# Attention scores from stacked bf16 parts or from fp32 strips, in a two-layer kernel on one core

## What is computed

```python
# "raw" attention (kind A): 16 heads of width 8
att = jnp.einsum('nqd,nkd->nqk', qm, km)
att = jax.nn.softmax(att, axis=-1)
att_out = jnp.einsum('nqk,nkd->nqd', att + batch_pos, vm)
# "cell" attention (kind B): 8 heads of width 16, in six nodes one after the other
scores = jnp.einsum('bqhd,bkhd->bhqk', qh, kh) / jnp.sqrt(dh)
attn = jax.nn.softmax(scores, axis=-1)
ctx = jnp.einsum('bhqk,bkhd->bqhd', attn, vh).reshape(B, S, d)
```

## Time and profile before

| | us |
|---|---|
| median of 3 runs (1749.43 to 1760.54) | 1758.84 |
| the profiled execution, its own time | 1754.03 |
| span in that profile, first to last instruction | 1752.0 |
| busy: TensorE (PE) / VectorE (DVE) | 1246.1 / 1222.1 |
| busy: ScalarE (ACT) / GpSimd (POOL) | 770.1 / 465.1 |
| mean granted TensorE clock | 0.827 of full speed |

### The profile page before, as it was taken

How to read it: one execution, slowest core, us unless ns; L and a number is a source line. 1 busy time by engine, 2 the same in 40 slices (tenths; PEclk the granted TensorE clock), 3 DMA queues, 4 the chain that set the end, 5 groups by cost and what they waited for, 6 DMA issues and landing times.

```text
span 1752.0 us, 25484 instructions
## 1 busy us (share of the span) xinstructions
PE 1246.1 (71%) x8542; PEld 816.5 (47%) x8542; DVE 1222.1 (70%) x2380; ACT 770.1 (44%) x1684; POOL 465.1 (27%) x399
## 2 busy tenths in 40 slices
PE   6544577568878687869876886868786988478327
PEld 5222244334655356635663465535563566246216
DVE  4212345499859975898679875898589866976774
ACT  0222255354626464446435462646444644443322
POOL 4002002323230413142223323042324222421160
PEclk9966699686988798868987798869896898579759
DMA  4125523512470346133451247034623344122102
GB/s 144 25 34 55 60 37 44 64 17 46 59 119 6 37 80 90 39 36 68 59 78 22 52 62 108 5 37 80 87 42 36 66 56 66 18 55 62 44 1 63
DMA packets 151439, 94.52 MB, mean 54 GB/s; under 512 B 43104, under 2 KB 133232, under 8 KB 151184
## 3 DMA queue, kind: packets, MB, share of 16 engines
q1 hardware_dynamic: 151312, 92.90, 34.2%
HBM read 44.88 MB, written 3.42 MB: 28 GB/s over the span
## 4 chain that ended last, share of the span: by engine, by line
PE 37%; DVE 31%; DMA 10%; issue 10%; ACT 6%; SPq 5%; POOL 1%; DVEq 0%; POOLq 0%; ACTq 0%
DVE hb L1498 8%; PE px L985 5%; PE scores_t L825 5%; PE px L997 5%; PE ps L805 5%; PE attn_out L838 4%; DVE rowmax_B L1347 4%; DMA w_e<-in_w_e 4%; DVE hb L1493 4%; DMA qks<-parts_b 3%; SPq L589 2%; DMA qks<-maxrow_B 2%; ACT probs L1091 2%; DVE rowmax_A L1347 2%; DVE work L1467 2%
## 5 line engine op out<-in xcount | busy, mean ns | idle before, releaser
L1347 DVE TENSOR_REDUCE rowmax_B<-ps 128x2 f32<-128x512 f32 x384 | 246.4, 684 | 139.7 <-PE ps L805 138.5
L1091 ACT ACTIVATE probs<-scores_t 128x512 f32<-128x512 f32 x512 | 286.9, 594 | 100.6 <-PE scores_t L825 98.5
L805 PE MATMUL ps<-qks 96*128 96x256 bf16 x768 | 166.0, 326 | 154.1 <-DMA qks<-parts_b 95.0
L825 PE MATMUL scores_t<-qks 98*128 98x256 bf16 x768 | 162.8, 318 | 43.5 <-ACT probs L1091 31.2
L997 PE MATMUL px<-ze,w_e 128*128 128x256 f32 x512 | 144.9, 417 | 59.0 <-DMA w_e<-in_w_e 54.6
L1633 POOL TENSOR_TENSOR parts_b<-rem_b,parts_b 128x256 bf16<-128x256 f32 x96 | 90.7, 948 | 347.5 <-ACT parts_b L1059 347.3
L805 PEld LDWEIGHTS ps<-qks 96*128 96x128 bf16 x768 | 69.3, 109 | 228.4 <-DMA qks<-parts_b 101.2
L1498 DVE TENSOR_TENSOR_SCAN hb<-da,hb 128x1024 f32<-128x1024 f32 x64 | 164.1, 2565 | 2.2
L1584 DVE SCALAR_TENSOR_TENSOR work<-hb,px 128x512 f32<-128x512 f32 x128 | 86.1, 682 | 112.8 <-ACT hb L1218 112.7
L1083 ACT ACTIVATE maxrow_B<-ps 8x256 bf16<-8x256 bf16 x96 | 35.5, 370 | 243.6 <-PE ps L813 242.4
L985 PE MATMUL px<-w_e,work 128*128 128x128 f32 x1024 | 134.9, 288 | 8.0 <-DVE work L1584 7.6
(11 more groups left out here) (277 smaller groups left out, 2324.9 us busy)
## 6 DMA issues: line engine op xcount, KB each, us to landing
qks<-parts_b SPq DMA_DIRECT2D x288, 128.0 KB, 4.9
w_e<-in_w_e SPq DMA_DIRECT2D x128, 256.0 KB, 3.2
stage_a<-parts_a SPq DMA_DIRECT2D x96, 64.0 KB
pos<-t_scr SPq DMA_DIRECT2D x8, 264.0 KB, 13.8
qks<-maxrow_B SPq DMA_DIRECT2D x96, 4.0 KB
probs<-in_b_we_t SPq DMA_DIRECT2D x1, 1280.0 KB, 6.0
x_in<-in_x SPq DMA_DIRECT2D x8, 128.0 KB, 3.1
v_scr<-va_fm SPq DMA_DIRECT2D x8, 128.0 KB, 12.8
```

The source lines that it names most:

```text
L805: mm = pe.matmul(o[:, qc * L:(qc + 1) * L], q(STACK, qc * P, P), k(STACK, 0, L), start=True, stop=True)
L825: mm = pe.matmul(scores_t[unit % 2][:, kc * L:(kc + 1) * L], k(STACK + 2, kc * P, P), q(STACK + 2, 0, L), start=True, stop=True)
L1091: act.activation(probs[:, group % 2, h % 4, :, :].rearrange("p a b -> p (a b)"), scores_t[unit % 2][:, :], ACT.Exp).then_inc(s_exp, 1)
L1347: dve.tensor_reduce(out=top[:, :, h], in_=parts_of(bank(b, ("max", kind, n))), axis=AX, op=ALU.max).then_inc(max_done[kind].of(b), 1)
```

## The change

Queries and keys stay fp32. Four heads lie in four strips of 32 partitions (16 features used in kind B, 8 in kind A, and the next row holds the maxima on the query side and -1 on the key side), and eight fp32 products with 16 (or 8) rows, issued strip after strip, fill four PSUM banks: four heads at once. The projections therefore make 2 x 128 columns in place of 128. The parts, the remainders, the stacking DMAs and the reordering copies are gone; so are the bf16 parts of the maxima. For the raw attention the projections go to DRAM and come back as eight DMAs in pieces of 64 bytes. VectorE reduces two heads (128x1024) at a time, ScalarE takes the exponential of two heads at a time. The four banks (`strips`, two tiles of two banks) serve the maxima and the scores in turn, and there is one set of them: `take_strips` waits for both readers of the product before. `px` is gone: layer 1 takes its banks from the three `ps`, in one round with the attentions. All places in the order are new.

```diff
-    CELL += [("q", _c), ("q1", _c), ("q2", _c), ("stack", _c, 0), ("stack", _c, 1), ("stack", _c, 2)]
-    CELL += [("max", "B", _c * BH + _h) for _h in range(6)] + [("rows", "B", 2 * _c)]
-    CELL += [("max", "B", _c * BH + _h) for _h in range(6, BH)] + [("rows", "B", 2 * _c + 1)]
-    CELL += [("score", "B", _c, _h) for _h in range(BH)]
+    CELL += [("q", _c)]
+    for _g in (2 * _c, 2 * _c + 1):
+        CELL += [("max", "B", _g), ("top", "B", _g, 0), ("top", "B", _g, 1), ("rows", "B", _g)]
+    for _g in (2 * _c, 2 * _c + 1):
+        CELL += [("score", "B", _g), ("exp", "B", _g, 0), ("exp", "B", _g, 1)]
...
-        scores_t = [ctx.enter_context(nc.psum_tensor(f"scores_t{i}", [P, 512], F32)) for i in range(2)]
+        strips = [ctx.enter_context(nc.psum_tensor(f"strips{i}", [P, 2 * 512], F32)) for i in range(2)]
...
-        px = [ctx.enter_context(nc.psum_tensor(f"px{i}", [P, 512], F32)) for i in range(2)]
...
+            def a_write(b):
+                sp.wait_ge(*qkv_a_done.at(b, 1))
...
+                sp.dma_start(bass.AP(tensor=a_scr.tensor, offset=0, ap=[[L, P], [A_PITCH * L, 3], [1, L]]), qkv_a[:, :, :]).then_inc(a_written.of(b), 16)
...
+            def gathered(i, first, heads, features):
+
+                return bass.AP(tensor=a_scr.tensor, offset=i * A_PITCH * L + 16 * first, ap=[[16, heads], [L, 16 * features], [1, 16]])
...
+                for g in range(A_GROUPS):
+                    for i, x in enumerate((qs["A"][g], ks["A"][g])):
+                        sp.dma_start(x[:, :].rearrange("p (c r) -> p c r", c=CB), gathered(i, AG * g, AG, STRIP)).then_inc(stacked_a.of(b), 16)
...
+                for g in range(2):
+                    mm = pe.matmul(o[:, g * L:(g + 1) * L], wmk[:, c, g, :], nt[:, b % 2, nk, :], start=True, stop=True)
+                mm.then_inc(s_ps, 1)
...
+            def take_strips(b, *phase):
+
+                at = STRIP_AT[(b, *phase)]
+                if at:
+                    user, was, kind, g = STRIP_LIST[at - 1]
+                    for i in range(2):
+                        if was == "max":
+                            pe.wait_ge(*top_done[kind].at(user, 2 * g + i))
+                        else:
+                            pe.wait_ge(s_exp, EXP_AT[user, kind, g, i] + 1)
+
+            def strip(tiles, b, kind, g, j, rows, first, n):
+                part, span = slice(STRIP * j, STRIP * j + rows), slice(first, first + n)
+                return tiles["B"][b % 2][part, g % 2, span] if kind == "B" else tiles["A"][g][part, span]
...
+                take_strips(b, "max", kind, g)
                 for qc in range(2):
-                    mm = pe.matmul(o[:, qc * L:(qc + 1) * L], q(STACK, qc * P, P), k(STACK, 0, L), start=True, stop=True)
-                mm.then_inc(s_ps, 1)
+                    for j in range(4):
+                        o = strips[j // 2][:, (2 * (j % 2) + qc) * L:(2 * (j % 2) + qc + 1) * L]
+                        mm = pe.matmul(o, strip(qs, b, kind, g, j, rows, qc * P, P), strip(ks, b, kind, g, j, rows, 0, L), start=True, stop=True)
+                mm.then_inc(s_strips, 1)
...
+            def exp(b, kind, g, i):
+                strips_ready(act, b, "score", kind, g)
...
+                act.activation(probs[:, group % 2, 2 * i:2 * i + 2, :, :].rearrange("p h a b -> p (h a b)"), strips[i][:, :], ACT.Exp).then_inc(s_exp, 1)
...
+                dve.tensor_reduce(out=rowmax[kind][:, b % sides_n, k % 2, 2 * i:2 * i + 2, :], in_=strips[i][:, :].rearrange("p (h q t) -> p h q t", h=2, q=2),
+                                  axis=AX, op=ALU.max).then_inc(top_done[kind].of(b), 1)
...
-            def reorder(b):
...
-                pool.tensor_copy(qsa[0:PARTS * AW, :].rearrange("p (n r c) -> p n r c", n=AH, c=CB), src).then_inc(reordered.of(b), 1)
```

More of the change, by code:

```diff
@@ L35 @@
 GELU_A, GELU_B = 0.7978845608028654, 0.044715
-CHUNK = 4
 RING = 3
@@ L90 @@
 ON = {
-    "sync": "load stack rows t_rows a_stack pos v_write v_read o_write o_read weights store",
+    "sync": "load rows t_rows a_write a_stack pos v_read o_write o_read weights store",
     "tensor": "prep_t q k v max rows score values post_b post_a ctx node aproj values_a gather wo_y ab_t ff_y "
               "z_t inproj bcdt state x2 h_t ffn ffn_out router expert expert_y",
-    "scalar": "prep_t q q1 k k1 v rows score out ctx node aproj a1 values_a gather ab_t "
+    "scalar": "prep_t q k v rows exp out ctx node aproj values_a gather ab_t "
               "z_t inproj xc bcdt sp_u sp_z state h_t ffn ffn_t router expert",
-    "vector": "prep_stats prep_apply q1 k1 a1 max post_b post_a end_y end_apply end_x wo_y wo_apply ff_y ff_apply "
+    "vector": "prep_stats prep_apply top post_b post_a end_y end_apply end_x wo_y wo_apply ff_y ff_apply "
               "n0_stats n0_apply n1_stats n1_apply n2_stats n2_apply inproj conv xc bc sp_u sp_z state y x2 ffn ffn_t ffn_out router rank expert expert_y",
-    "gpsimd": "prep_root xn_bo q2 k2 a2 reorder end_root end_scale wo_root ab_t ff_root att n0_root n1_root n2_root n0_apply conv sp_z state x2",
+    "gpsimd": "prep_root xn_bo end_root end_scale wo_root ab_t ff_root att n0_root n1_root n2_root n0_apply conv sp_z state x2",
 }
 START = {
[L104 to L107, removed]
+    "cell": [0, 24256, 48447, 72656, 96862, 121064, 145226, 169427],
+    "side": [814, 25027, 49237, 73418, 97637, 121825, 146010, 170205],
+    "raw": [193, 24399, 48624, 72826, 97064, 121238, 145411, 169627],
+    "one": [212, 24423, 48614, 72824, 96997, 121183, 145339, 169276],
 }
@@ L116 @@
+        "one": [130550, 134861, 138785, 142283, 143837, 145068, 145232, 145663, 146602],
     },
     "tensor": {
-        "cell": [-13098, -12947, -11035, -11004, -10774, -10451, -10198, -10171, -9965, -9628, -9218, -8915, -8743, -8653, -8243, -8242, -7928, -7369,
[6 rows of a table removed]
[L125 to L128, removed]
@@ L512, in hybrid_layers @@
         OUT_AT = {x: i for i, x in enumerate(OUT_LIST)}
-        REM_LIST = {which: [(b, s[1]) for b, s in order("vector") if s[0] == which + "1"] for which in "qk"}
         CTX_LIST = [(b, s[1]) for b, s in order("vector") if s[0] == "post_b"]
-        assert [k for k in UNIT] == [(b, *s[1:]) for b, s in order("scalar") if s[0] == "score"]
+        assert [(*x[:1], *x[2:], i) for x in STRIP_LIST if x[1] == "score" for i in range(2)] == list(EXP_AT)
         assert [k[:3] for k in GROUP if k[3] == 0] == OUT_LIST
@@ L771, in keys @@
                 o = take(b, ("k", c))
-                pe.matmul(o[:, 0:L], wmk[:, c, :], nt[:, b % 2, nk, :], start=True, stop=True).then_inc(s_ps, 1)
+                for g in range(2):
+                    mm = pe.matmul(o[:, g * L:(g + 1) * L], wmk[:, c, g, :], nt[:, b % 2, nk, :], start=True, stop=True)
+                mm.then_inc(s_ps, 1)
             def values_in(b, c):
@@ new lines, in scored, with queries @@
+            def scored(b, c):
+                if c:
+                    strips_ready(act, b, "score", "B", 2 * c - 1)
+                elif b >= 2:
+                    strips_ready(act, b - 2, "score", "B", 2 * NODES - 1)
+            def queries(b, c):
+                ready(act, b, ("q", c))
+                scored(b, c)
+                for g in range(2):
+                    act.activation(qs["B"][b % 2][:, g, :], bank(b, ("q", c))[:, g * L:(g + 1) * L], ACT.Identity, bias=bias_q[:, c, g:g + 1]).then_inc(q_done.of(b), 1)
@@ L1061, in values_in, with keys @@
+            def keys(b, c):
+                ready(act, b, ("k", c))
+                scored(b, c)
+                for g in range(2):
+                    act.activation(ks["B"][b % 2][:, g, :], bank(b, ("k", c))[:, g * L:(g + 1) * L], ACT.Identity, bias=bias_k[:, c, g:g + 1]).then_inc(k_done.of(b), 1)
             def values_in(b, c):
@@ L1753, in layouts @@
     put("be", f["L0_ffn_be"].T)
+    put("minus", -(np.arange(P) % STRIP == BW).astype(np.float32)[:, None])
     put("a_bq", f["L0_attn_bq"][cd][:, None])
```

523 lines of the change are left out of this document (211 added, 312 removed), and 13 rows, old and new, of the table PLACES.

## The result

The changed kernel takes 1826.66 us (median of 4 runs, 1824.24 to 1831.10) against 1758.32 us: a ratio of 1.040, 95% interval 1.036 to 1.044. It is 4% slower where the prediction said 1680 us and faster. The profiled execution has a span of 1827.1 us, 75 us more than the one before.

A forecast was written before the change was run, and what follows sets the result against it. No engine was taken as full: DVE bounds the scan, PE the next stretch, with waits between. From 1754 us, setup +9, fill -50 and seven intervals of -5 (-35) gave 1678, stated as 1680 us, range 1610 to 1950.

The forecast's parts named there:

- DMA: Per interval: weight wait gone -10, or moved to the rows of maxima +5; -5 taken, plus -4 for PE's stack waits.
- third rival: No change: the DMA convoy takes from the rows what it gave the weights, fill only -30; about 1755 us, chance 0.12.
- a period above 195 us: Sequence-to-sequence distance that would prove the prediction wrong; near 184 us was expected, 189.5 us before.
- first rival: Slower: one set of strips makes PE's queue wait for DVE or ACT at hand-overs; 1825 us, chance 0.25.
- second rival: Slower: strips load weights one after another, 1.9 us a phase; 1835 us, chance 0.17.
- Fill and setup: Start of the run: fill -50 us (-20 to -80) from faster nodes; setup +9 (0 to +15).
- near 300 us: Sign for the fill: the successor of line L1467 starts there in the first sequence, 360.4 us before.
- PE: Added products, scores and array shape changes: +16.4 us per sequence, counted at about half, +8.
- DVE: Larger reductions, no remainders or small instructions: -17 us per sequence (-13 to -19), counted as -7.
- Copy lock: POOL's reordering copy goes, with the 5 us in which DVE and PE stood: -5 per sequence, the surest term.
- Hand-overs: PE waits for reductions or exponentials to free the strips: 0.25 us a phase, +8 per sequence (0 to +42).
- The sum: Per interval -5 us, seven times -35; with setup +9 and fill -50, 1754 becomes 1678, given as 1680.

The follow-up runs named there:

- e1: Changed kernel with the 64-byte pieces made once, on the write to scratch, and strips loaded in 1 KB rows: 1668.31 us, ratio 0.951 to the kernel before.
- e7: Pieces-once kernel (e1) with the wait for the strips' readers split in halves, two heads per reduction or exponential: 1654.85 us, ratio 0.942.
- e3: Changed kernel with the spatial attention's strips loaded for sequence 0 alone, seven of eight loads left out: 1665.44 us, ratio 0.952.
- e11: Pieces-once kernel (e1) measured again without edit: 1663.24 us, ratio 0.950.
- e6: Pieces-once kernel (e1) with each maxima phase's 16 matmul instructions issued twice: 1805.75 us, ratio 1.026.
- e8: Kernel before with the twelve spatial stack loads and POOL's reorder copy done for sequence 0 alone: 1676.79 us, ratio 0.954.
- e9: Kernel before with POOL's reorder copy done for sequence 0 alone, the twelve stack loads kept: 1727.0 us, ratio 0.984.
- e10: Changed kernel with the four loads of queries in 1024 pieces of 128 bytes instead of 2048 of 64: 1772.04 us, ratio 1.010.
- e4: Kernel before with eight unused loads of 2048 64-byte pieces added ahead of the attention output's write: 2144.0 us, ratio 1.223.
- e5: Changed kernel with the strip loads moved from SP's list to POOL's, as 32 loads of 512 pieces: 2172.3 us, ratio 1.237.

## Why the prediction was wrong, by its steps

**The step that failed: DMA.** The prediction saw the eight loads, their 64-byte pieces, and that they stand ahead of the rows of chunks 10 and 11. It wrote "Gone would be -10; moved to the rows, which PE needs in its order, could be +5. I take -5." The wait for the weights did go: of 54.6 us in all before, 6.8 per sequence (not 10), 0.4 us are left. What came in its place is 17.5 us per sequence (139.8 over 8). So by these two waits alone the term is about +10.7, not -5. Neither end of the term, -10 or +5, is worked out from the loads. The prediction asked where the convoy stands; it has no number of pieces times a price in it, and nothing on how long SP needs to get through eight issues. That length, 27.4 us, is what the runs showed in its place.

The whole price of the pieces is larger than the wait: 22.2 us per interval in the middle, between the changed kernel's period (200.2) and that of e1, (1053.5 - 519.4)/3 = 178.0 us. Of these 17.5 are the wait. The third rival had this mechanism, priced at "no change"; it was off by its size. The prediction's own sign of being wrong, a period above 195 us, came true. That the first rival (1825) and the second (1835) name nearly the measured time is luck: what they charge it to, the hand-overs and the loading of weights, is not what costs (e1, e7 and below).

Part of the price is the clock. Windows of one period each: changed kernel, then e1.

```profile
952.90:1157.70 204.80, 165.58 (x1343) 111.51 (x1342) 129.95 (x209) 92.34 (x177) 32.18 (x33) 0.82 0.15 32
```

```profile
874.70:1053.50 178.80, 155.82 (x1342) 107.22 (x1342) 130.34 (x210) 92.15 (x177) 32.26 (x33) 0.90 0.14 37
```

The same instructions keep PE busy for 165.6 us at a granted clock of 0.82 and for 155.8 us at 0.90; in the period before each of these it is 158.1 us at 0.86 and 153.3 us at 0.91. The 16 instructions of the scores right after the wait take 2.09 us, at a granted clock of 0.50, 1.2 GHz; 16 at 1.00, 2.4 GHz, take 1.15 us (848.92 us in the same trace). So the 17.5 us of waiting are not all that the idle stretch costs.

**Fill and setup: -41 predicted (-50 and +9), -2 measured, -25 to -34 without the heap.** The heap stands in the fill of the first sequence too. By the prediction's own sum the reciprocal of the first sequence would start at 360.4 - 41 = 319 us; the "near 300 us" that it names as a sign left out the setup and 10 us more. Without the heap it starts at 335.6 us in e1, 336.1 in e3 and 326.7 in e11. A part of the miss is setup, +9 predicted. The last setup product (L725 before, L690 in e1) starts 14 us later, by the chain in order of time:

```profile
47.91 1.90 PE ps L725 x2
```

```profile
61.89 1.23 PE ps L690 x2
```

The upper end of that term, +15, would have been the better choice. With 14 us of setup taken off, the rest of the fill is 39 us shorter in e1 and 48 in e11, against 50. The nodes of the first sequence are nearly as fast as I said, 24 to 26 us: by the chain of e1, the maxima of three successive nodes begin at

```profile
75.62 1.12 PE strips L787 x16
...
103.42 1.19 PE strips L787 x16
...
129.01 1.19 PE strips L787 x16
```

27.8 and 25.6 us apart. What makes the remaining 2 to 11 us was not tried; e1 and e11 are one kernel and differ by 9 us here.

**PE: +16.4 us per sequence.** A period went from 148.1 us of PE (mean of two windows, clock 0.84) to 161.8 us in the changed kernel (158.1 and 165.6, mean clock 0.84 too): +13.8 at the same clock. In e1 it is 154.6 us at 0.90. The engine term is about right, a little high. Its weight, one half, is not borne out: e6 says 0.8 or more, for the kernel without the heap and with the reservation above. A phase of 16 strip instructions was put at 1.04 us, the trace has 1.15 us with the drain:

```profile
827.65 1.15 PE L784 MATMUL strips<-ks_a,qs_a 8*128 8x256 f32 x16 [0.55 <-ACT probs L1066]
```

**The second rival is excluded.** Strips load their weights side by side: on the page the 1536 loads of L784 have a mean of 216 ns, 332 us if they were serial, and keep the loader busy for 81.8 us, a fourth. A phase takes 1.15 us, where the rival needed 1.9 and the prediction put 3.4 for nothing overlapped.

```profile
L784 PEld LDWEIGHTS strips<-ks_b,qs_b 16*128 16x128 f32 x1536 | 81.8, 216 | 64.7 <-issue 40.6
```

The Trainium skill, page "TensorE: Matmul & The Clock Gate", section "Measured speedup vs the span model", gives 3.07 times for four row strips. The trace agrees: 3.4 us (the prediction's estimate) over 1.15 us is 3.0 times. The reading of a serial load that made the rival does not hold for loads into different strips.

**DVE: -17 us.** 152.1 to 130.3 us is -22; the copy's lock is in it. The old kernel without the convoy (e8) has 147.7 and 147.0 us of DVE in a period, so the change's own part is -17. The two sizes under it hold: reductions 1219 ns, exponentials 1021 ns, against 1.22 and 1.02 us.

**Copy lock: -5 per interval.** 4.2 us by e9. In the changed kernel the 128x2 instruction of the earlier trace rows is down to a mean of 0.34 us. The term that was called the surest held.

**Hand-overs: +8, between 0 and +42; the first rival.** In e1 PE waits 92.5 us in front of strips for reductions and exponentials, (40.8 + 27.8 + 14.0 + 6.4 + 3.5)/8 = 11.6 us per sequence, less than the 130 us in all that I had set as the sign for the rival. The half waits leave 34.0 of them (e7) and give back 6 to 13 us, 1 to 2 us per interval. So a value near +8 is possible at most, a smaller one more likely, and the rival is excluded.

**The sum.** Without the heap the kernel takes 1663 to 1668 us where 1680 was predicted. By the profile of e1: fill and setup -25 (-41 predicted), intervals -7.1 each (175.8 against 182.9; -5 predicted), tail -5 (nothing predicted). That the total comes so near is partly luck: the fill gave less than I said, the intervals and the tail more. In the changed kernel the interval is +11.9 us. One term of five microseconds turned the sign. (In the sum of "all bad ends", 39 us per interval takes VectorE's and the stack waits' terms at their middle; nothing else hangs on it.)

## What to carry to other kernels

A DMA of many small pieces is paid by whatever stands behind it in its issuer's order: count its pieces, take the price of an issue from the middle of a batch and not from its first or from a lone one, and multiply it by the batch. Where a layout has to be turned on the way through DRAM, turning it once, on the write, and reading it back in whole rows can pay; here that is 6144 pieces of 64 bytes per sequence against 18432, and 9% of the time, though most of the 18432 held rows that nobody uses. And when a term looks like a convoy that only changes places, ask first how long it is.

## What the runs showed of the hardware

- An issue on SP's queue right behind a load of 128 KB took 0.43 us where that load was 128 rows of 1 KB (e1), 2.3 us for 1024 pieces of 128 bytes (e10), 3.7 to 3.9 us for 2048 pieces of 64 bytes (changed kernel), and 6.0 us for the same from DRAM to DRAM (e4); the first of a batch took 0.56 us, and an ordinary write behind the batch 3.70 us. In the changed kernel the DMA engines' busy share was 0.41 meanwhile.
- POOL needed about 2.55 us for each DMA of 512 pieces (e5), 80 us for what SP issued in 27.4 us.
- Four heads' fp32 products in strips of 32 rows run side by side with their weight loads: 16 instructions in 1.15 us at a granted clock of 1.00, 2.09 us at 0.50, after an idle stretch of 18 us.
